# A graph network's spread stage: the tile of parts that each product reads is copied to a fixed place by GpSimd

## What is computed

```python
x = layernorm(x + L0(x, edges)); x = layernorm(x + L1(x, edges)); x = layernorm(x + L2(x, edges))
# L3, for each edge (src, dst):
h = relu(concat(x[src], x[dst]) @ W1 + b1)
interaction = h @ W2 + b2
gated = interaction * sigmoid(interaction @ Wg + bg)
pooled = segment_sum(gated, src) / max(counts(src), 1)
x = layernorm(x + pooled)
```

## Time and profile before

| | us |
|---|---|
| median of 3 runs (lowest, highest) | 3859.66 (3855.13, 3863.49) |
| the profiled execution, its own time | 3853.53 |
| its span in the trace | 3851.8 |
| the stage, first product to the end of the last | 2242.2 to 2613.0 |

### The profile page before, as it was taken

One profiled execution on the slowest core, in us unless ns is written; L12 is line 12 of the kernel. 1 busy time (PEld: TensorE's weight loads), 2 busy tenths in 40 slices (PEclk: granted clock), 3 DMA queues, 4 the chain that ended last, 5 costly groups with the idle time before them and its releaser, 6 DMA issues.

```text
span 3851.8 us, 144496 instructions
## 1 busy us (share of the span) xinstructions
PE 3108.9 (81%) x46724; PEld 2623.8 (68%) x46725; DVE 2702.2 (70%) x7781; ACT 1951.9 (51%) x4306; POOL 1615.6 (42%) x1691
## 2 busy tenths in 40 slices
PE   5986246777888869989989867778999999999996
PEld 2443123433444459889879867777999999999996
DVE  9998989999999950420320276666777777777777
ACT  7975035777888830000000033336666666666665
POOL 1000068468777774057777620003333333333331
PEclk9987568988999989999999967778999999999998
DMA  1000022222233269899889657774333333333332
GB/s 49 5 3 1 11 86 98 92 104 84 102 108 112 102 250 338 285 317 318 308 265 312 205 169 248 249 246 125 96 97 94 97 96 95 96 97 96 94 97 67
DMA packets 219825, 550.28 MB, mean 143 GB/s; under 512 B 67881, under 2 KB 129573, under 8 KB 193855
## 3 DMA queue, kind: packets, MB, share of 16 engines
q1 hardware_dynamic: 161315, 480.18, 36.8%
q0 software_dynamic: 51616, 66.64, 6.7%
q10 hardware_dynamic: 6716, 1.12, 0.2%
HBM read 400.09 MB, written 151.85 MB: 143 GB/s over the span
## 4 chain that ended last, share of the span: by engine, by line
PE 56%; DVE 21%; issue 11%; DVEq 6%; ACT 4%; DMA 1%; POOL 1%; ACTq 0%; SPq 0%; PEldq 0%; POOLq 0%
PE ps L2089 17%; DVE x L636 10%; PE ps L2284 8%; PE ps L2064 8%; PE ps L2296 8%; PE ps L2250 7%; DVE rows L762 6%; PE ps L2275 3%; PE ps L2264 2%; ACT stage L1784 1%; DVE x L1068 1%; DVEq L1060 1%; DVEq L1057 1%; PE ps L2007 1%; DVEq L1056 1%
## 5 line engine op out<-in xcount | busy, mean ns | idle before, releaser
L2064 PE MATMUL ps<-rows 128*128 128x448 bf16 x2272 | 632.6, 411 | 220.9 <-DVE rows L762 155.3
L1548 POOL DMA_INDIRECT x<-b_rows_all,gidx x416 | 403.4, 970 | 785.6 <-DVE x L1068 655.9
L762 DVE TENSOR_SCALAR rows<-iota_c,x 128x448 bf16<-128x448 bf16 x2272 | 679.5, 373 | 15.1 <-PE ps L2064 14.2
L2064 PEld LDWEIGHTS ps<-rows 128*128 128x128 bf16 x2272 | 331.1, 146 | 522.4 <-issue 403.0
L1904 ACT ACTIVATE x<-ps,b1col 64x256 f32<-64x256 f32 x920 | 431.9, 469 | 391.6 <-PE ps L2275 331.2
L1452 POOL DMA_INDIRECT quad_keys<-key_quads,key_at x416 | 451.9, 1086 | 127.3 <-issue 126.5
L1784 ACT ACTIVATE stage<-ps 128x448 bf16<-128x448 f32 x700 | 385.5, 554 | 205.5 <-PE ps L2064 196.5
L2284 PE MATMUL ps<-w2cat,x 128*128 128x128 f32 x3680 | 487.2, 276 | 0.0
L2089 PE MATMUL ps<-x,rows 128*128 (+1 forms) x13230 | 419.2, 195 | 60.2 <-issue 39.8
L1501 POOL DMA_INDIRECT dst_ids<-ids,slot x416 | 411.0, 988 | 126.8 <-issue 126.8
L2296 PE MATMUL ps<-x 128*128 128x65 f32 x3680 | 462.2, 269 | 0.1
(11 more groups left out here) (406 smaller groups left out, 4068.9 us busy)
## 6 DMA issues: line engine op xcount, KB each, us to landing
rows<-adjacency SPq DMA_DIRECT2D x90, 1024.0 KB
adjacency<-stage SPq DMA_DIRECT2D x50, 1568.0 KB
x<-adjacency SPq DMA_DIRECT2D x60, 1024.0 KB
b_rows_all<-x SPq DMA_DIRECT2D x116, 512.0 KB, 3.5
x<-src_rows SPq DMA_DIRECT2D x460, 128.0 KB, 3.1
rows<-adjacency SPq DMA_DIRECT2D x90, 544.0 KB
x<-adjacency SPq DMA_DIRECT2D x60, 544.0 KB
x<-dst_ids SPq DMA_DIRECT2D x116, 256.0 KB, 4.3
```

The lines of the kernel that those rows point to most:

```text
L762: ins = e.tensor_scalar(hot_dst[:, k, :], iota_c[:], rel_col[:, bass.ds(i0 + k, 1)], None, ALU.is_equal)
L1548: e.indirect_dma_start(out=BGT[:, s, :, :].rearrange("p j f -> p (j f)"), out_offset=None, in_=b_rows_all, in_offset=bass.IndirectOffsetOn ...
L2064: e.matmul(psf[:, bass.ds(at_bank, WIN)], hot_src[:, k // HOTS, :, k % HOTS], hot_dst[:, k % HOTS, :], start=False, stop=False, skip_group ...
```

## The change

GpSimd gets a new function, `copy_tiles`. For each item it loads the tile's number from `spread_tab` (four at a time), waits until the products of the item four before it are done (`spread_done`), and copies the 192 columns of that tile's parts from `blk_rows` to place i mod 4 of `AT`, counting `tile_copied`. TensorE's products read `AT[:, u, ...]`, a fixed address; its loads of `spread_tab` and its address arithmetic are gone, and it waits for `tile_copied` beside `id_hot_ready`. The copies of 64 items (four rounds of GpSimd's loop of 16) come ahead of each of the seven `split_a` groups, those of the last 16 items behind them. GpSimd starts on all this only when the tables have landed and the last `split_b` is done.

```diff
@@ block.gpsimd
-            for g in range(EG):
-                split_a(g)
+            spread_tiles = [e.alloc_register(f"spread_tile{n}") for n in range(4)]
+
+            def copy_tiles(r, n):
+
+                e.load(spread_tiles, spread_tab[0:1, bass.ds(r * 16 + 4 * n, 4)])
+                for u in range(4):
+                    t = e.snap(spread_tiles[u], min_val=0, max_val=NTP - 1)
+                    e.wait_ge(spread_done, r * 16 + (4 * n + u + 1))
+                    e.tensor_copy(AT[:, u, :], blk_rows[:, bass.ds(t, 1), :].rearrange("p a f -> p (a f)")
+                                  ).then_inc(tile_copied, 1)
+
+            e.wait_ge(tables_in, 16 * 5)
+            e.wait_ge(dve, mark["b_split"])
+            for g in range(EG + 1):
+                with e.Fori(4 * g, min(4 * g + 4, SUPER // 4)) as r:
+                    for n in range(4):
+                        copy_tiles(r, n)
+                if g < EG:
+                    split_a(g)
@@ block.tensor
-            tiles = [e.alloc_register(f"spread_tile{n}") for n in range(8)]
             hot = ID_HOT.rearrange("p s (c j) -> p s j c", j=G)
             with e.Fori(0, SUPER // 2) as r:
-                e.load(tiles, spread_tab[0:1, bass.ds(r * 8, 8)])
                 for n in range(2):
                     for u in range(4):
-                        t = e.snap(tiles[4 * n + u], min_val=0, max_val=NTP - 1)
+                        e.wait_ge(tile_copied, r * 8 + (4 * n + u + 1))
                         e.wait_ge(id_hot_ready, r * 8 + (4 * n + u + 1))
                         if u % 2 == 0:
                             e.wait_ge(spread_copied, r * 4 + (2 * n + u // 2 + 1))
                         for j in range(G):
                             for k in range(3):
                                 ins = e.matmul(ps[:, 4 + u // 2, (u % 2 * G + j) * D:(u % 2 * G + j + 1) * D], hot[:, u, j, :],
-                                               blk_rows[:, bass.ds(t, 1), k * D:(k + 1) * D].rearrange("p a f -> p (a f)"),
+                                               AT[:, u, k * D:(k + 1) * D],
                                                start=(k == 0), stop=(k == 2))
```

More of the change, by code:

```diff
@@ L427, in build_gnn @@
         tables_in = sem("tables_in")
+        tile_copied = sem("tile_copied")
         bx_turned = sem("bx_turned")
```

## The result

| | median us (lowest, highest) | runs |
|---|---|---|
| before | 3861.57 (3855.13, 3870.14) | 4 |
| after | 3823.84 (3817.43, 3829.61) | 4 |

A forecast was written before the change was run, and what follows sets the result against it. TensorE set the pace, standing 1.56 us between rounds. Start at 2240.2, 58 rounds of 5.30 (307.4) and 22 for the split groups moved the end from 2613.0 to 2569.6, 43.4 us less: 3816 us, range 3778 to 3850.

The forecast's parts named there:

- The forecast case: Whole stage: rounds of about 5.30 us and pauses for the split groups, 3800 to 3832 us; chance 0.55.
- the chain of the stores: ScalarE's copy, store and landing before an `EV` place is reused: 5.64 or 4.96 us a round.
- at most the 1.56 us a round: TensorE's stand between rounds, the most that removing its table load and address operations was to be worth.
- the largest of three terms: A round's cost: TensorE's products 5.12 or 3.28 us, stores 5.64 or 4.96, VectorE's matrices 3.9.
- the middle of 5.64 and 4.96: Forecast round of 5.30 us, between a super's two copies 1.28 us apart and 0.60 apart.
- The pauses: TensorE stands while GpSimd runs a split group: 3.9 us six times, 1.7 for the seventh; 22 us taken.
- a sign of being wrong: GpSimd's copies, forecast at 0.35 us, taking over 0.47 us would show the prediction wrong.
- ScalarE's clearing: Stage start: clearing `total` lets 2.0 us through of about 3 gained, so the stage can start at 2240.2.
- 1, the clock: TensorE in the stage: clock rises to 2.4 GHz for good, rounds of 4.7 us, 3782 us; chance 0.15.
- 2, slower stores: Store landings in the stage: stores become the bound and slow down, rounds of 5.8 us, 3847 us; chance 0.17.
- 3, turns: GpSimd and VectorE exclude each other for whole operations, 0.84 us an item, 3899 us; chance 0.10.
- 4, the bank: TensorE's gap is the copy of the bank, not the load; rounds stay 6.31 us, 3869 us; chance 0.03.

The follow-up runs named there:

- four places: The store buffer `EV` given four places instead of two: kernel before 3860.4 us, changed kernel 3761.7 us, fixed tile 3738.5 us.
- either part alone: Kernel before, two `EV` places, products reading tile 0 but one, address operations gone: 3812.5 us; or table load moved ahead of the loop: 3812.7 us.
- split operations apart: Changed kernel, two `EV` places, with `split_a` cut into 35 single operations, one behind the copies of every 12 items: 3809.9 us.
- first version with both edits: Changed kernel with four `EV` places and `split_a` cut into single operations, one behind every 12 items, table numbers still loaded four at a time: 3794.1 us.
- fixed tile: Kernel before without TensorE's table load and address operations, every product reading tile 0, output wrong: 3809.3 us, second run 3813.1 us.
- the load alone: Kernel before with four `EV` places, table load kept every round, one product using its address and the rest reading tile 0: 3782.7 us.
- the address operations alone: Kernel before with four `EV` places, table load once ahead of the loop, address operations kept for every item: 3786.3 us.
- with neither: Kernel before with four `EV` places, no table load or address operations on TensorE, every product reading tile 0: 3738.5 us.

## Why the prediction was right, and where it was off

- **Time and sign.** Forecast 43.4 us less, 3816, measured 37.7 less, 3823.8. The forecast case (3800 to 3832) is the one that came, and its mechanism too.
- **The bound.** Right that TensorE set the pace, that the copy of the bank was booked in the place of something else, and that the chain of the stores is next: 142.4 us of waits. Wrong in size on what goes: "at most the 1.56 us a round". With four places the round fell by 6.38 - 4.15 = 2.23, since the address operations, which the forecast gave no price, draw the products out by 1.2 us beside the load's stand of 1.4. The sum did not suffer, because it took the largest of three terms and that was the stores. With two places taking away either part alone gives nearly the whole gain (stages of 323.8 and 325.6).
- **The round.** Forecast 5.30; the 52 rounds without one of the six long pauses took (335.1 - 54.2)/52 = 5.40, 5.8 us in all. The term that was small is the landing: 4.0 us instead of the 3.5 of the earlier trace rows, with transfers at 0.79 of the engines' time, not the 0.88 that was worked out. That was the bound for slower landings (0.5 us later, round 5.8), but the rest of the chain ran short: products wait, so the two copies of a super follow each other at once, 0.49 us apart in the median, where the middle of 5.64 and 4.96 had in effect taken 0.94. The chain with both is 0.76 + 4.0 + 0.1 + 0.49 = 5.35. That two errors of half a microsecond cancelled is luck; that this chain is the bound is not.
- **The pauses.** Forecast 22 us. The six rounds with a pause sum to 54.2 us, 9.03 each, 3.63 over 5.40: 21.8. The small seventh one is inside the 52 rounds (6.60 us where it stands). TensorE's stand was forecast at 3.9 us and is 4.1 in the timeline above. The run with split operations apart gives 17.0 for them.
- **The copy.** Forecast 0.35 alone and hidden. Its minimum is 0.34, and 0.35 is what it takes where it meets no matrix; its median is 0.535, since it ends behind VectorE's matrix as the matrix ends behind it. That is over the 0.47 that the forecast named as a sign of being wrong. That GpSimd "pays little", 0.07 us, was read from operations of 1.2 us and does not hold for a short one. It cost nothing all the same (rounds 4.21 and 4.15), so the sign was ill chosen: it took the copy's drawn-out time for something to be added to the matrix's. The matrix's median, 0.56, was as forecast.
- **The table load on GpSimd.** Forecast 0.29 us beside the engine, which is a load of one number in another stage; the load of four took a median of 0.68, and 0.32 at the least. In the changed kernel it is hidden in the steady part; it is what spoiled the first version with both edits.
- **The start.** Forecast 2.0 us earlier, with ScalarE's clearing as the bound. From the mark to the first product are 15.4 us before and 12.3 after, 3.1 less (the other kernels with `split_a` at the start have 16.6 to 17.1, those with copies 12.3 to 12.8). TensorE starts at 2247.09, ahead of the clearing's end (2244.73 + 3.25 = 2247.98), so the clearing is no bound:

```profile
2244.73 3.25 ACT L1889 ACTIVATE stage<-zero_col 128x3250 f32<-128x3250 f32 x1
...
2247.09 6.28 PE L2266 MATMUL ps<-x 128*128 128x64 bf16 x144 [6.69 <-DVE x L1038]
```

  The first product waits for the count of `spread_copied`, which stands behind the clearing in ScalarE's program; it had been given by 2247.09, 0.9 us before that activation ended.
- **The rivals.** 1, the clock: it rose to 0.91, and with a fixed tile to 0.96 (0.93 in its second run), but rounds did not fall to 4.7, as the stores bound them. 2, slower stores: in part, 5.40 of 5.8. 3, turns: with four places an item took 0.53 us against 0.84. Its rule, in the Trainium skill's "SBUF — State Buffer", section "Who interferes with whom", is that of VectorE in a two-port mode and GpSimd the second engine fully blocks for the whole instruction of the first. That both engines are held fits the durations here (0.56 for 0.49, 0.53 for 0.34) better than the forecast's reading did. That the whole instruction is held does not: a copy ended 0.20 us behind the matrix, less than its own 0.35, and a matrix 0.28 behind the copy, less than its own 0.49, so a good part of each operation lies outside what is blocked. 4, the bank: rounds did not stay.

The sum as measured, from the mark: rounds 5.8 us over, pauses 0.2 under, the start 1.1 earlier than forecast, and the stage before counted 0.7 too long (to 2613.0, where the last product begins at 2612.3): 43.4 - 5.8 + 0.2 + 1.1 - 0.7 = 38.2, for the 38.0 in the profiles.

## What to carry to other kernels

Before an engine's gap is taken out, list what each of its neighbours would need for the same work, and work out the chain through every ring of two buffers: here it held the gain to 38 us, and two more places of an idle buffer were worth 60 more. A gap can have several causes, and another bound can hide what each is worth: take them out one at a time with that bound moved away, and read each one's price from the engine's own time and not from the length of a round that something else may still set. And fine pieces of side work are not always better than coarse ones: each piece brings its handovers, and they must fit in the ring's slack as well.

## What the runs showed of the hardware

- A load of four table numbers on GpSimd took 0.32 to 1.54 us (median 0.55 to 0.82 in four versions) while VectorE worked; a load of one number took 0.29 in the edge stage, and one of twelve 1.61. That VectorE's operations delay it was not shown apart.
- Address operations on TensorE's sequencer stretched 96 products from 3.46 to 4.64 us at full clock. Its load of eight table numbers took 1.17, 1.27 and 1.37 us in the median in three versions with products in flight, 0.59 at the least, and a stand of 1.4 us a round came with it.
- A GpSimd copy of 0.35 us and a VectorE matrix of 0.49 that overlapped ended 0.20 and 0.28 us behind each other: both were held, neither for the other's whole length.
- DMA engines at a share of 1.00 moved 381 GB/s, and a store then took 6.4 us to land, for 3.5 at 0.74. The list of DMA issues of the fixed tile with four places:

```profile
b_rows_all<-x SPq DMA_DIRECT2D x44, 512.0 KB, 6.4
```

- The granted clock followed neither TensorE's busy share nor its stands alone. Between 2300 and 2500 us it was 0.77 before, with products 0.78 of the time and stands of 1.45 us a round; 0.98 with the load alone, at 0.71 and 1.38; 1.00 with the address operations alone, at 0.96 and 0.21; 1.00 with neither, at 0.85; and 0.91 in the changed kernel, at 0.66. Two profiles of the fixed tile with two places had 0.96 and 0.93 between 2270 and 2570 us.
